# Output projection, second norm and routing in 13 tiles of 125 rows where they were 16 of 100, with attention's result in a ring of 250 columns

## The chip, the cores and the metric

The kernel runs on 1 core of one Trainium2 chip. The metric is device time in microseconds (us); lower is better. Before the change it is 1721.82 us, the median of 3 runs (1720.84 to 1722.42).

## What is computed

A gated cross-attention block and a mixture of experts behind it, for 16 batches (B) of 100 rows (S) of 512 features (D), all in float32:

```python
x = x + tanh(g_xattn) * attention(layernorm(x), ctx)   # 16 heads of 32, 722 context rows per batch
    # q = xn @ Wq.T + bq ; k, v = ctx @ Wk.T + bk, ctx @ Wv.T + bv
    # softmax(q k.T / sqrt(32) + mask) @ v, heads side by side, then @ Wo.T + bo
x = x + tanh(g_ffn) * moe(layernorm(x))
    # gates = softmax(xn @ gate_w + gate_b), the best 2 of 8 experts per row
    # expert: gelu(xn @ w1 + b1) -> gelu(. @ w2 + b2) -> . @ w3 + b3, weighed by its gate
```

From the output projection on, nothing depends on the batch that a row belongs to: projection, residual, norm and routing are done row by row.

## The kernel before, in words

**Precision.** The large products are made of three passes of matmuls: each float32 operand is split into a high and a low part (`PRODUCTS`: high*high, high*low, low*high). ScalarE (ACT) writes the high parts, VectorE (DVE) the low ones.

**Two halves.** The first half of the program (0 to about 999 us) is attention with projection, norm and routing; the second runs the experts over rows that routing has scattered to `expert_in_rows` in HBM. The amount of work in the second half is fixed by constants. Most of one expert (the "early" one, 256 rows) is run in the last part of the first half.

**Bodies.** The first half is a prologue, `first_body` (b = 0), fourteen times `body` (b = 1 to 14; b = 14 is a small variant), and `last_body` (b = 15). All are unrolled, and the order of each engine's work is written by hand. Body b has four groups. Group g computes the scores of the four heads of g (`scores`, line 791), has the softmax run on DVE and ACT (`score` L1470, `exps` L1145), meanwhile finishes the four heads of the group before (`attend`, L814 and L817), runs "units" of filler work on TensorE (PE), and transposes the probabilities (`transpose_probs`, L803) in two pairs. Units are the keys (K, 12 matmuls, L736) and values (V, 12 matmuls of 512 columns, L750) of this and the next batch, the queries (Q, L773), and, once for each body, Y (`project_o`, L830, the output projection of the batch before: 12 matmuls of 512 columns) and CNT (`count_pairs`, L855 and L856, four small matmuls). Units alternate between two PSUM banks; a unit waits until the unit two before it has been read out (`emptied`).

**Attention's result.** After `attend`, `scale_o` on DVE multiplies the bank by the reciprocal sums into `o_t` (L1492). It stands inside `scored_around`, between the second and the third of four `score` instructions. Only at g = 2 (for the three tiles of g = 0, 1, 2 at once, 300 columns) and at g = 3 (100 columns) is `o_t` split into `o_high` (L1497) and `o_low` (L1499).

**The round of a tile.** One round follows each batch, in the next body: Y; on DVE `residual`, `residual_add` with norm statistics, `norm_out`, eight router dots (`dots`, L1535: one for each expert, each of which overwrites its row of router weights, so POOL loads that row again, `load_router`, L543, four slots), `biased`, `less_max`, `choose` (L1559 to L1567), `place`, `carry`, `aim`; on ACT `rstd_start`, `second_copy`, `route_exps`; on POOL `scatter` (L563). SP stores `x_res` (L645) and loads the next (L657). For the last two tiles the logits come from PE instead of the dots. In DVE's program `values_out` of V2 (L1451) stands behind `choose`, and CNT on PE waits for `either` (L1567). In `last_body`, `early_raw` (L1635) on DVE reads out the early expert's first layer, behind the `scored_around` of the group.

**POOL at the start.** POOL fills the experts' regions in HBM with eight DMAs of 3.3 MB (L555), and after five of them issues the first four router loads. Then it follows the dots of tile 0.

## Time and profile before

| | |
|---|---|
| median of 3 runs | 1721.82 us |
| profiled execution, its own time | 1722.78 us |
| its span | 1720.9 us |
| outside the span | 1.88 us |
| PE busy, share of the span | 99% |
| DVE, ACT, POOL | 70%, 54%, 10% |
| granted TensorE clock | full in every slice of the span |
| in the chain that ended last | PE 88%, DVE 2%, ACT 1% |

The profile is of one execution. A row of the timeline gives an instruction's start and its duration; consecutive matmuls overlap in it, so that the time that a group of matmuls takes is the distance from its first start to the first start of what follows. The chain of waits is followed back from the last instruction, at each step to what released it; there the pieces don't overlap and their lengths can be added.

### The profile page before, as it was taken

What the parts mean: (1) busy time and instruction counts of PE and PEld (TensorE: products, weight loads), DVE (VectorE), ACT (ScalarE), POOL (GpSimd) and SP (SyncE); (2) the same over time, 40 slices, a digit from 0 to 9 for tenths busy, and PEclk for the clock granted to TensorE, in tenths of its full rate; (3) what the DMA queues carried; (4) which work ended last, traced back from release to release, by engine and by line L of the source; (5) the groups of instructions that cost most, each with busy time, mean ns of one, the idle gap of its engine ahead of it and who ended that gap; (6) DMA issues with size and microseconds to landing.
All of it is one profiled execution on the core that took longest, in us unless ns stands there. A gap on an engine that the chain in (4) does not pass through costs nothing.

```text
span 1720.9 us, 40335 instructions
## 1 busy us (share of the span) xinstructions
PE 1704.8 (99%) x15462; PEld 1509.2 (88%) x15462; DVE 1209.4 (70%) x2807; ACT 931.6 (54%) x1652; POOL 180.1 (10%) x271
## 2 busy tenths in 40 slices
PE   9999999999999999999999999999999999999997
PEld 8888888898889888988898878777899999999997
DVE  5677777777777777777775575566677777777773
ACT  4655656565556555655555454455545555545551
POOL 2010110111011101110110100000011010110100
PEclk9999999999999999999999999999999999999999
DMA  9982322222222222221215499998666666667662
GB/s 296 371 316 77 83 89 78 66 83 88 67 77 83 88 68 77 83 89 46 80 33 182 174 367 384 348 353 285 200 214 214 212 205 206 209 224 226 219 197 49
DMA packets 128181, 292.72 MB, mean 170 GB/s; under 512 B 19610, under 2 KB 42842, under 8 KB 128040
## 3 DMA queue, kind: packets, MB, share of 16 engines
q1 hardware_dynamic: 104616, 225.46, 38.8%
q0 software_dynamic: 23424, 65.30, 12.8%
q8 instruction: 98, 1.61, 0.4%
q14 instruction: 43, 0.35, 0.1%
HBM read 244.04 MB, written 46.66 MB: 169 GB/s over the span
## 4 chain that ended last, share of the span: by engine, by line
PE 88%; DVE 2%; issue 1%; ACT 1%; DMA 0%; POOLq 0%; POOL 0%; DVEq 0%; ACTq 0%
PE bank_rows L2301 21%; PE bank_rows L750 13%; PE bank_rows L736 12%; PE bank_rows L2316 7%; PE bank_rows L803 6%; PE bank_rows L2355 5%; PE bank_rows L791 4%; PE bank_rows L814 3%; PE bank_rows L2341 3%; PE bank_rows L2382 3%; PE bank_rows L830 2%; PE bank_rows L773 2%; PE bank_rows L894 2%; DVE probs L1470 1%; PE bank_rows L2393 1%
## 5 line engine op out<-in xcount | busy, mean ns | idle before, releaser
L1145 ACT ACTIVATE probs<-probs,neg_max 100x726 f32<-100x726 f32 x256 | 228.9, 896 | 168.1 <-DVE neg_max L1470 168.1
L2545 DVE TENSOR_TENSOR w_low<-stage,w_high 128x1024 fp32r<-128x1024 f32 x176 | 213.3, 1223 | 35.5 <-ACT w_high L2449 35.0
L1470 DVE CUSTOM_DVE_ANT_0 probs<-bank_rows,mask_sb 100x726 f32<-100x726 f32 x256 | 222.9, 909 | 16.4 <-PE bank_rows L791 14.8
L2449 ACT ACTIVATE w_high<-stage 128x1024 fp32r<-128x1024 f32 x176 | 183.9, 1057 | 33.4 <-DMA stage<-in_L_ffn_w 33.2
L2472 ACT ACTIVATE gelu<-bank_rows,biases 128x256 f32<-128x256 f32 x176 | 82.3, 474 | 216.4 <-PE bank_rows L2301 211.7
L1151 ACT ACTIVATE p_t<-bank_rows 122x1200 f32<-122x1200 f32 x128 | 146.4, 1168 | 95.8 <-PE bank_rows L803 95.8
L2301 PE MATMUL bank_rows<-h_high,w_high 128*128 128x256 f32 x704 | 196.5, 279 | 0.0
L2301 PE MATMUL bank_rows<-h_low,w_high 128*128 128x256 f32 x704 | 196.5, 279 | 0.0
L2301 PE MATMUL bank_rows<-h_high,w_low 128*128 128x256 f32 x704 | 196.5, 279 | 0.0
L736 PE MATMUL bank_rows<-ctx_high,wk_high 128*128 128x360 f32 (+1 forms) x512 | 175.7, 343 | 3.3 <-DVE v_even L1451 2.1
L736 PE MATMUL bank_rows<-ctx_low,wk_high 128*128 128x360 f32 (+1 forms) x512 | 167.8, 328 | 0.0
L736 PE MATMUL bank_rows<-ctx_high,wk_low 128*128 128x360 f32 (+1 forms) x512 | 167.2, 326 | 0.0
L750 PE MATMUL bank_rows<-wv_high,ctx_high 128*120 128x512 f32 (+1 forms) x384 | 154.5, 402 | 0.3 <-DVE k_low L1444 0.3
L750 PE MATMUL bank_rows<-wv_high,ctx_low 128*120 128x512 f32 (+1 forms) x384 | 151.4, 394 | 0.0
L750 PE MATMUL bank_rows<-wv_low,ctx_high 128*120 128x512 f32 (+1 forms) x384 | 151.3, 394 | 0.0
L803 PEld LDWEIGHTS bank_rows<-ident,probs 100*120 100x120 f32 (+1 forms) x1536 | 138.8, 137 | 10.3 <-ACT probs L1145 1.4
L803 PE MATMUL bank_rows<-ident,probs 100*120 100x100 f32 (+1 forms) x1536 | 143.8, 249 | 0.2
L2301 PEld LDWEIGHTS bank_rows<-h_high,w_high 128*128 128x128 f32 x704 | 132.3, 188 | 0.0
L2301 PEld LDWEIGHTS bank_rows<-h_low,w_high 128*128 128x128 f32 x704 | 132.3, 188 | 0.0
L2301 PEld LDWEIGHTS bank_rows<-h_high,w_low 128*128 128x128 f32 x704 | 132.3, 188 | 0.0
L1122 ACT ACTIVATE k_high<-bank_rows,bk_sb 128x362 fp32r<-128x362 f32 (+1 forms) x128 | 71.9, 562 | 94.2 <-PE bank_rows L736 93.9
L2559 DVE CAST h_high<-gelu 128x256 fp32r<-128x256 f32 x176 | 51.7, 294 | 99.5 <-ACT gelu L2472 99.5
(245 smaller groups left out, 3869.9 us busy)
## 6 DMA issues: line engine op xcount, KB each, us to landing
stage<-in_L_ffn_w SPq DMA_DIRECT2D x240, 512.0 KB, 4.7
plain_w<-in_L_ffn_w SPq DMA_DIRECT2D x15, 2048.0 KB, 12.4
expert_in_rows<-filling POOLq DMA_DIRECT2D x8, 3341.0 KB, 25.2
router_rows<-in_gate_rows POOLq DMA_DIRECT2D x112, 200.0 KB, 3.4
ctx_raw<-in_ctx SPq DMA_DIRECT2D x16, 720.0 KB, 4.9
ctx_raw<-in_ctx SPq DMA_DIRECT2D x15, 724.0 KB, 4.3
xs_sb<-expert_in_rows SPq DMA_DIRECT2D x11, 514.0 KB, 5.4
b_sb<-in_L_ffn_b SPq DMA_DIRECT2D x19, 256.0 KB, 4.9
```

The lines of the kernel that those rows point to most:

```text
L736: last = nc.tensor.matmul(bank[:, 0:size], wk_hl[a][:, c, m * P:(m + 1) * P], ctx_t[b][half][:, c, :], start=(c == 0 and s == 0), stop=(c ...
L750: last = nc.tensor.matmul(bank[0:rows, :], ctx_t[a][half][:, c, off:off + rows], wv_hl[b][:, c, :], start=(c == 0 and s == 0), stop=(c == ...
L803: last = nc.tensor.transpose(slots_of(q)[0:rows, i // 2, i % 2 * S:(i % 2 + 1) * S], probs[:, q, off:off + rows], ident[0:S, 0:S])
L1145: nc.scalar.activation(p, p, ACT.Exp, bias=neg_max[:, h:h + 1], scale=-1.0, accum_out=exp_sum[:, h:h + 1]).then_inc(probs_ready, 1)
L1151: nc.scalar.activation(p_t[:, q:q + 2, :, :].rearrange("t q (k i) s -> t (q k) (i s)", k=PIECES), slots[0:TT, PIECES * q:PIECES * (q + 2), ...
L1470: nc.vector.tensor_tensor_reduce(out=pieces(probs[:, q, :]), in0=slots_of(q)[0:S, :, 0:PIECE], in1=pieces(mask_sb[:]), scale=-1.0, scalar= ...
L2301: last = nc.tensor.matmul(mm_bank[m % 4][:, 0:BLOCK], w[a][:, k, m * P:(m + 1) * P], src[c][:, k, :], start=(k == 0 and s == 0), stop=(k = ...
L2316: last = nc.tensor.matmul(y_bank[t][:], h_hl[1][a][:, k, t * P:(t + 1) * P], w_hl[2][c][:, k, :], start=(k == 0 and s == 0), stop=(k == HT ...
L2355: last = nc.tensor.matmul(second_bank[half][:], small_h1[a][:, k, :], w_hl[1][c][:, k, cols], start=(k == 0 and s == 0), stop=(k == HT - 1 ...
L2449: nc.scalar.activation(hi, src, ACT.Copy).then_inc(chunk_hi[which], 1)
L2472: nc.scalar.activation(gelu[:, m % 2, :], mm_bank[m % 4][:, 0:BLOCK], ACT.Gelu, bias=bias_of(n, layer, m)).then_inc(g_done, 1)
L2545: nc.vector.tensor_tensor(lo, src, hi.bitcast(F32), ALU.subtract).then_inc(chunk_lo[which], 1)
```

## The change

Rows of batches 0 to 14 (1500 rows) are taken as 12 tiles of 125 rows; batch 15 is tile 12, with 100 rows. A tile is done in the first body after which its rows are complete (`tile_of`): bodies 1, 6 and 11 have none. There Y, CNT and everything of the round on DVE, ACT and POOL are left out, and V4 takes Y's place on PE. The output of attention goes to a ring of 250 columns for each feature tile. A batch that crosses the ring's end (2, 7 and 12) is written in two pieces of 50 columns. `scale_o` splits its own 100 columns at once, for each g. POOL's first router loads come behind all eight region fills, since one of the four slots now lies where `filling` is. Some tensors get another place in SBUF. Tensors of a tile have 125 partitions where they had 100.

```diff
+R = 125
+NR = (B - 1) * S // R + 1
+FIRST_TILES = NR - 2
+RING = 2 * R
+def tile_of(body):
+    if body == B:
+        return NR - 1
+    done, last = (S * b // R for b in (body, body - 1))
+    return done - 1 if done > last else None
+
+def ring_pieces(b):
+    at, first = S * b % RING, min(S, RING - S * b % RING)
+    return [(at, 0, first)] + ([(0, first, S - first)] if first < S else [])
...
+    if 0 < body < B - 1 and tile_of(body) is None:
+        _names = tuple(u for u in _names if u not in ("Y", "CNT"))
...
-    o_hl = [place(f"o_{n}", [P, DT, S], F32R) for n in ("high", "low")]
+    o_hl = [place(f"o_{n}", [P, DT, RING], F32R) for n in ("high", "low")]
...
     (on_gpsimd)
         def load_router(e):
             k = e % ROUTER_SLOTS
-            pool.dma_start(router_rows[k][:], gw_rows[e:e + 1, :].broadcast_to([S, D])
+            pool.dma_start(router_rows[k][:], gw_rows[e:e + 1, :].broadcast_to([R, D])
                            ).then_inc(router_loaded[k], 16)
...
             elif e == len(FILL_AFTER):
                 pool.wait_ge(mask_loaded, 64)
-                for k in range(ROUTER_SLOTS):
-                    load_router(k)
...
-        pass_router(0, E)
         pool.wait_ge(regions_filled, 16 * E)
-        scatter(0)
-        with pool.Fori(1, IN_ROWS - 1) as b:
-            pass_router(b, E)
-            scatter(b)
+        pool.wait_ge(spare_filled, 32 * TPB)
+        for k in range(ROUTER_SLOTS):
+            load_router(k)
+        with pool.Fori(0, IN_ROWS - 1) as t:
+            pass_router(t, E)
+            scatter(t)
...
     (on_sync)
-        def load_after(b, t):
+        def load_after(t):
             stored(t)
-            sp.dma_start(x_res[:], batch_rows(x, b)).then_inc(xres_loaded, 16)
+            sp.dma_start(x_res[0:rows_in(t + 1), :], tile_rows(x_rows, t + 1)).then_inc(xres_loaded, 16)
...
     (on_tensor)
         def project_o(body, cs=range(DT)):
             bank, ready = bank_for(body, "Y", cs[0] == 0)
-            t = body - 1
+            t = tile_of(body)
+            n, at = rows_in(t), R * t % RING
             if cs[0] == 0:
                 pe.wait_ge(wo_split, 2)
-                pe.wait_ge(o_split, 2 * t + 1)
+                pe.wait_ge(o_split, DT * (body - 1) + DT - 1)
             for c in cs:
                 if c == DT - 1:
-                    pe.wait_ge(o_split, 2 * t + 2)
+                    pe.wait_ge(o_split, DT * (body - 1) + DT)
                 for step, (a, w) in enumerate(PRODUCTS):
-                    last = nc.tensor.matmul(bank[0:S, :], o_hl[a][:, c, :], wo_hl[w][:, c, :],
+                    last = nc.tensor.matmul(bank[0:n, :], o_hl[a][:, c, at:at + n], wo_hl[w][:, c, :],
                                             start=(c == 0 and step == 0), stop=(c == DT - 1 and step == 2))
...
         def body(b, odd, t, n):
             scores(b, 0)
-            attend(b, t, 1 - odd, 3)
+            attend(b, b - 1, 1 - odd, 3)
             values(b, 3)
-            project_o(b)
+            if t is not None:
+                project_o(b)
+            else:
+                values(b, 4)
             transpose_probs(b, 0)
             transpose_probs(b, 1)
-            values(b, 4)
+            if t is not None:
+                values(b, 4)
             values(b, 5)
...
-            count_pairs(b, t)
+            if t is not None:
+                count_pairs(b, t)
...
     (on_vector)
         def scale_o(body, b, g):
             bank, done = take(body, f"A{g}")
             dve.wait_ge(r_copied, DT * b + g + 1)
-            nc.vector.tensor_tensor(o_t[:, g, :], bank[:, 0:S], r_sb[:], ALU.mult).then_inc(done, 1)
-            if g >= DT - 2:
-                bank, fills = unit(body, f"A{g}")
-                dve.wait_ge(emptied[bank], fills)
-                gs = slice(0, DT - 1) if g == DT - 2 else slice(DT - 1, DT)
-                nc.vector.tensor_copy(o_hl[0][:, gs, :], o_t[:, gs, :]).then_inc(o_hi, 1)
-                dve.wait_ge(o_hi, 2 * b + g - 1)
-                nc.vector.tensor_tensor(o_hl[1][:, gs, :], o_t[:, gs, :], o_hl[0][:, gs, :].bitcast(F32),
-                                        ALU.subtract).then_inc(o_split, 1)
+            nc.vector.tensor_tensor(o_t[:], bank[:, 0:S], r_sb[:], ALU.mult).then_inc(done, 1)
+            bank, fills = unit(body, f"A{g}")
+            dve.wait_ge(emptied[bank], fills)
+            for at, first, size in ring_pieces(b):
+                nc.vector.tensor_copy(o_hl[0][:, g, at:at + size], o_t[:, first:first + size]).then_inc(o_hi, 1)
+            dve.wait_ge(o_hi, o_pieces_to(b, g))
+            for at, first, size in ring_pieces(b):
+                made = nc.vector.tensor_tensor(o_hl[1][:, g, at:at + size], o_t[:, first:first + size],
+                                               o_hl[0][:, g, at:at + size].bitcast(F32), ALU.subtract)
+            made.then_inc(o_split, 1)
...
         def body(b, odd, t, n):
-            residual(b, t)
-            residual_add(b, t)
+            if t is not None:
+                residual(b, t)
+                residual_add(b, t)
...
-            dots(t, (5, 6, 7))
-            biased(t)
-            less_max(t)
+            if t is not None:
+                dots(t, (5, 6, 7))
+            if t is not None:
+                biased(t)
+                less_max(t)
```

The same `if t is not None` stands before `norm_out`, the other `dots`, `choose`, `place`, `carry` and `aim` on DVE, and before `rstd_start(1, t)`, `second_copy` and `route_exps` on ACT. In `last_body` and behind it the tile is `tile_of(15)` = 11 and then 12. The experts' half only has the counts in its waits changed (16 tiles to `NR` = 13).

## Rows read from the trace of the kernel before

**Rows 1.** The page, busy time by engine (us, share, instructions).

```profile
PE 1704.8 (99%) x15462; PEld 1509.2 (88%) x15462; DVE 1209.4 (70%) x2807; ACT 931.6 (54%) x1652; POOL 180.1 (10%) x271
```

**Rows 2.** Waits of PE, longest in total: waiter, released by, us, times, longest.

```profile
PE bank_rows L736 <- DVE v_even L1451: 2.1, 2, 1.6
...
PE bank_rows L814 <- DVE k_low L1444: 1.1, 1, 1.1
```

**Rows 3.** Chain of waits in body 12: start, us, what.

```profile
733.46 2.77 PE bank_rows L830 x12
736.23 2.06 PE bank_rows L803 x24
738.29 5.60 PE bank_rows L750 x24
```

**Rows 4.** PE's timeline around CNT in body 8: start, us, instruction.

```profile
606.12 2.22 PE L803 MATMUL bank_rows<-ident,probs 100*122 100x100 f32 x24
608.18 0.26 PE L855 MATMUL bank_rows<-either,before 100*100 100x8 f32 x2
...
608.52 0.43 PE L736 MATMUL bank_rows<-ctx_high,wk_high 128*128 128x360 f32 x1
```

**Rows 5.** Windows from one Y to the next: stretch, length, busy times, clock, DMA.

```profile
95.60:156.05 60.45, 58.64 (x643) 51.36 (x642) 43.92 (x125) 34.25 (x67) 6.45 (x10) 1.00 0.70 238
502.43:560.50 58.07, 57.97 (x641) 51.03 (x640) 43.71 (x123) 34.16 (x67) 6.61 (x10) 1.00 0.27 78
618.13:675.83 57.70, 57.70 (x642) 50.92 (x641) 43.71 (x123) 34.17 (x67) 6.61 (x10) 1.00 0.26 79
```

**Rows 6.** Router loads: chain in body 1; DMA issues, median landing; all waits.

```profile
128.08 7.21 DMA router_rows<-in_gate_rows
...
router_rows<-in_gate_rows POOLq DMA_DIRECT2D x112, 200.0 KB, 3.4
...
  DMA router_rows<-in_gate_rows: 14.5, 15
```

**Rows 7.** DVE's timeline, `scale_o` and the score behind it, at g = 3, 1, 2.

```profile
442.71 0.26 DVE L1492 TENSOR_TENSOR o_t<-bank_rows,r_sb 128x100 f32<-128x100 f32 x1 [0.43 <-ACT r_sb L1132]
...
443.44 0.91 DVE L1470 CUSTOM_DVE_ANT_0 probs<-bank_rows,mask_sb 100x726 f32<-100x726 f32 x1
...
473.04 0.26 DVE L1492 TENSOR_TENSOR o_t<-bank_rows,r_sb 128x100 f32<-128x100 f32 x1 [0.44 <-ACT r_sb L1132]
473.22 0.90 DVE L1470 CUSTOM_DVE_ANT_0 probs<-bank_rows,mask_sb 100x726 f32<-100x726 f32 x1
...
486.53 0.26 DVE L1492 TENSOR_TENSOR o_t<-bank_rows,r_sb 128x100 f32<-128x100 f32 x1 [0.44 <-ACT r_sb L1132]
...
487.56 0.91 DVE L1470 CUSTOM_DVE_ANT_0 probs<-bank_rows,mask_sb 100x726 f32<-100x726 f32 x1
```

**Rows 8.** Timelines in group 2 of body 7: V1 read out, next K unit.

```profile
477.18 0.69 DVE L1451 TENSOR_TENSOR v_even<-bank_rows,bv_sb 120x512 f32<-120x512 f32 x1
...
478.72 0.41 PE L736 MATMUL bank_rows<-ctx_high,wk_high 128*128 128x362 f32 x1
```

**Rows 9.** Chain of waits at the end of body 7's group 3.

```profile
491.63 0.18 DVE either L1567
...
492.06 0.70 DVE v_even L1451
...
492.81 4.21 PE bank_rows L736 x24
```

**Rows 10.** PE's timeline, a wait in body 0 and one in body 15.

```profile
60.26 0.50 PE L750 MATMUL bank_rows<-wv_high,ctx_high 128*120 128x512 f32 x1 [0.35 <-DVE k_low L1444]
...
937.15 0.48 PE L878 MATMUL bank_rows<-early_xt,early_w 128*128 128x256 f32 x1 [0.16 <-DVE early_h L1635]
```

**Rows 11.** Timelines of ACT and PE in body 7: last copy, next scores.

```profile
449.88 1.16 ACT L1151 ACTIVATE p_t<-bank_rows 122x1200 f32<-122x1200 f32 x1
...
454.92 0.36 PE L791 MATMUL bank_rows<-k_high,q_high 32*100 32x242 f32 x4
```

More of the change, by code:

```diff
@@ L483, in pieces, with ln_rows @@
         return ap.rearrange("s (k t) -> s k t", k=PIECES)
+    def ln_rows(which, n):
+        return slice(0, S if which == 0 else rows_in(n))
     def early_bank(m):
@@ L706, in load_early @@
                 if which == 1:
-                    store(B - 2)
-                    load_after(B - 1, B - 2)
+                    store(NR - 2)
+                    load_after(NR - 2)
         for b in range(B - 1):
-            body(b, b - 1 if b > 0 else None, b + 1, b + 2 if b + 2 < B else None)
+            body(b, tile_of(b) if b > 0 else None, b + 1, b + 2 if b + 2 < B else None)
         load_early()
-        store(B - 1)
-        stored(B - 1)
+        store(NR - 1)
+        stored(NR - 1)
         sp.wait_ge(spare_filled, 32 * TPB)
@@ L1082, in on_tensor @@
         for b in range(1, B - 1):
[L1083 removed]
+            body(b, b % 2, tile_of(b), b + 1)
         last_body(B - 1, (B - 1) % 2)
@@ L1275, in body @@
             keys_high(b, n, *((1, 0) if odd else (0, 1)))
-            route_exps(t)
+            if t is not None:
+                route_exps(t)
             if b + 2 < B:
@@ L1389, in on_scalar @@
         for b in range(1, B - 1):
-            body(b, b % 2, b - 1, b + 1)
+            body(b, b % 2, tile_of(b), b + 1)
         last_body(B - 1)
@@ L1577, in place @@
+            route_then(t, k + 4, nc.vector.tensor_scalar(token[:], token[:], float(R), None, ALU.add))
         def place(body, t):
@@ L1759, in body @@
             keys_low(b, b, 3, 1)
-            dots(t, (0,))
+            if t is not None:
+                dots(t, (0,))
             if b + 2 < B:
-                ln_apply(0, b + 2, x_ln[:], xn[:], xn_ready)
+                ln_apply(0, b + 2, x_ln[:], xn[0:S, :], xn_ready)
             recips(b, 1)
@@ L1767, in body @@
                 ctx_low(n, 3)
-                dots(t, (1,))
+                if t is not None:
+                    dots(t, (1,))
                 values_out(b, 1 - odd, 0)
-                dots(t, (2,))
+                if t is not None:
+                    dots(t, (2,))
                 keys_low(b, n, 0, 0)
@@ L1775, in body @@
                 ctx_low(n, 3)
-                dots(t, (1,))
+                if t is not None:
+                    dots(t, (1,))
                 keys_low(b, n, 0, 0)
-                dots(t, (2,))
+                if t is not None:
+                    dots(t, (2,))
                 keys_low(b, n, 1, 0)
@@ L1796, in body @@
             keys_low(b, n, 3, 0)
-            choose(t)
+            if t is not None:
+                choose(t)
             values_out(b, 1 - odd, 2)
             recips(b, 3)
-            place(b, t)
-            carry(t)
-            aim(t)
-            if t == FIRST_BATCHES - 1:
+            if t is not None:
+                place(b, t)
+                carry(t)
+                aim(t)
+            if t == FIRST_TILES - 1:
                 pick_early()
@@ L1894, in on_vector @@
         for b in range(1, B - 1):
-            body(b, b % 2, b - 1, b + 1)
+            body(b, b % 2, tile_of(b), b + 1)
         last_body(B - 1)
```

287 lines of the change are left out of this document (158 added, 129 removed).

## The prediction

> **What bounds the kernel now.** I read four views in this order. The page first: PE is busy for 1704.8 of 1720.9 us, so only about 16 us are idle, and PE's own work is what a change has to shorten [rows 1]. Then PE's waits: they are few, and the largest two are for DVE [rows 2]. Then the stretch from one output projection to the next, body by body. An undisturbed body takes 57.70 us with PE busy for all of it, at the full granted clock (2.4 GHz); nine of the twelve from body 2 to 13 lie between 57.63 and 57.73, of which one stands here. Body 1 takes 60.45, body 8 58.07 [rows 5]. Last the chain of waits, which inside an undisturbed body consists of PE's units back to back: 12 matmuls of Y, the transposes, two units V [rows 3]. So a unit that is taken out of a body returns its whole length, as long as nothing that stood in its shadow comes out.
>
> **Three rounds less, on PE.** `tile_of` gives None where S*b//R doesn't grow: 0 at b = 0 and 1, 4 at b = 5 and 6, 8 at b = 10 and 11. So three bodies lose Y and CNT, and 13 rounds stay. Y runs from 733.46 to 736.23, 2.77 us [rows 3]: 3 * 2.77 = 8.31 us. That the other Y have 125 rows in place of 100 costs nothing by the rows: the 12 matmuls of V, with 120 result rows, take 5.60 / 2 = 2.80 us [rows 3], for the same 512 columns. CNT starts at 608.18 and the next unit at 608.52, 0.34 us [rows 4]; 3 * 0.34 = 1.02. The transposes before it take 608.18 - 606.12 = 2.06 [rows 4], the same as those that are followed by V [rows 3], so nothing is hidden in that border. Sum: **-9.33 us**.
>
> What covered what there: Y stood between V3 and the transposes, where the softmax of heads 0 to 3 has to get ready. V4 now takes its place, with the same length, so that cover stays. Behind the transposes two units stood before the next scores, now one. These scores wait for the last copy of the transposed probabilities, which ends at 449.88 + 1.16 = 451.04; they start at 454.92 [rows 11]. Taking 2.77 away leaves 454.92 - 2.77 - 451.04 = 1.1 us. The cover holds.
>
> The round's DVE, ACT and POOL work (some 40 instructions on DVE) also goes three times. I cost that at nothing: PE doesn't wait for it in an undisturbed body.
>
> **Body 1.** It is 60.45 - 57.70 = 2.75 us longer than its kind [rows 5]. The chain leads to a router row that took 7.21 us to land, where the median is 3.4 [rows 6]: the fills of the experts' regions keep the DMA engines busy (share 0.70 in this stretch, 0.26 later [rows 5]). DVE waits in the dots, and the waits of rows 2 are PE's behind it. Body 1 has no tile now, so it has no dots: **-2.75 us**. What is late next? Tile 0 is in body 2, whose dots stand behind its Y; that Y was at 156.05 [rows 5] and comes to about 150. The first four loads now wait for all the fills, which saves POOL the issue of four loads ahead of the last three fills; the DMA share falls from 0.70 over this body to about 0.27 in the later ones, and the router row of the chain landed at 128.08 + 7.21 = 135.3 [rows 6]. Even if the first loads were no earlier than that, they would be there 15 us before Y. Bounds: 0 (another wait takes its place) to -2.75; I take -2.75, since the chain goes through this load alone.
>
> **`scale_o` on DVE.** At g = 3 the step with a split of 100 columns takes 443.44 - 442.71 = 0.73 us from its start to the next score; at g = 1 without a split 473.22 - 473.04 = 0.18; at g = 2 with 300 columns 487.56 - 486.53 = 1.03 [rows 7]. After the change each is like g = 3. So the third and fourth scores come 0.55 us later at g = 0 and 1, and 0.30 earlier at g = 2. With two pieces (batches 2, 7, 12) there are two more short instructions; I estimate 0.2 us more, from an `either` of 0.18 us [rows 9] less the overlap of neighbours. Who waits for that:
>
> - Steady bodies, group 2 (g = 1): the chain on DVE runs on to V1's read-out, which ends at 477.18 + 0.69 = 477.87, and the K unit that needs that bank starts at 478.72: 0.85 us to spare in odd bodies [rows 8]. 0.55 leaves 0.30, and 0.75 in body 7 leaves 0.10. Cost nothing; upper bound 0.2 for each of 14 bodies, 2.8, if a stray pause falls there.
> - Group 3 (g = 2): V2's read-out stands behind `choose`. In body 7 it starts at 492.06 and K starts at 492.81 where it ends [rows 9]: PE waited. This is the excess of body 8 too, 58.07 - 57.70 = 0.37 [rows 5]; three bodies (7, 8, 12) have it, 0.9 us together. 0.30 us earlier takes about half of it: **-0.5 us** (bounds -0.9 and 0).
> - Body 0: PE waited 0.35 us for a `k_low` behind the softmax's scores [rows 10], so there the 0.55 comes through: **+0.5** (0 to 0.8).
> - Body 15: the early expert's first layer waits for `early_raw`, 0.16 us already [rows 10], once behind g = 0 and once behind g = 1. 2 * 0.55 = **+1.1** (0 to 1.7).
>
> **Other queues.** SP has three store-load pairs less and otherwise the order that it had. POOL scatters 125 rows thirteen times for 100 rows sixteen times. The experts' half has the same units. All at nothing: PE waits for none of them in rows 2.
>
> **The sum.** -8.31 - 1.02 - 2.75 - 0.5 + 0.5 + 1.1 = -10.98, say **-11.0 us**. The span goes from 1720.9 to 1709.9. The profiled execution took 1722.78, so its like would take 1711.8. It lay 0.96 above the median of 1721.82, so I forecast a median of **1710.8**.
>
> **A rule that speaks against the change.** A row of router weights lands in 3.4 us with 100 partitions [rows 6]. The Trainium skill, page "DMA: Bandwidth & Descriptors", section "Why a DMA increments its semaphore by 16 and not by 1", says that a DMA is spread over the largest number of engines up to 16 that divides its slowest dimension: 10 for 100 partitions, which by that rule is 5 for 125; it names an exception on trn2, where copies from GpSimd's queue use 16 engines with partitions/16, rounded up, on each. By the exception a router load has 8 rows on an engine where it had 7, and the sum stands; by the rule it takes about twice as long, and the next paragraph's first rival gives the time. No row here shows how many engines a transfer uses.
>
> **Rivals.**
>
> 1. *Router rows for 125 partitions land late (slower).* Dot 4 needs the load that dot 0 released, and so on; DVE waited 15 times for one, 14.5 us in all [rows 6], so this is a live edge in every body. Body 1 shows the price: 7.21 - 3.4 = 3.8 us late cost 2.75 on PE, so the first 1.05 are free. If all loads took 6.8 us, 3.4 late, each of 11 tiles in dots would cost 3.4 - 1.05 = 2.35: +25.9 - 11.0 = +14.9, 1736.7. It decides from a landing of 5.4 us, at which the 11.0 are used up (1.0 a tile). Against it: 250 KB for 200 is a quarter more of what is mostly a fixed time.
> 2. *The splits come through everywhere (slower).* 0.55 in two groups of 14 bodies is 15.4: -11.0 + 15.4 = +4.4, 1726.2. It decides from 11.0 / 28 = 0.4 us a group. Against it: 0.85 to spare [rows 8].
> 3. *Body 1 stays slow.* Something else waits for the crowded DMA engines: -8.2, 1713.6. The mask, context and x loads of body 1 share them, but the chain names none.
> 4. *The cover of the three short bodies fails* and PE waits for the softmax instead: -11.0 + 9.33 = -1.7, 1720.1. Against it: the 1.1 us above.
> 5. *The change doesn't do what it says*, the rounds aren't fewer or their units remain: also about 1720. The schedule worked out above speaks against it.
>
> **How the numbers follow.** Forecast 0.79, rival 1 0.03, rival 2 0.03, rival 3 0.10, rival 4 0.03, rival 5 0.02. The bounds of the forecast: all stalls gone and none added, -12.98, 1708.8; every upper bound taken, -8.31 - 1.02 - 2.75 + 0.8 + 1.7 + 2.8 = -6.8, 1715.0. This takes in rival 3. The runs of before spread over 1.6 us, so I add 0.8 at either end: 1708.0 to 1715.8. A difference under 0.2% (3.4 us) can't be told from none. Faster by more than that: 0.79 + 0.10 = 0.89; within it: 0.05; slower: 0.06.
>
> **What would show it.** 156 matmuls of Y in place of 192; the windows of bodies 6 and 11 near 54.6 us; body 1 also near 54.6; PE's waits for L1451 near 2 us gone; `o_high` with 128x100 in most rows; router rows landing near 3.5 us. I'm wrong if the other bodies rise above 57.8, if PE waits for `v_even`, `v_odd` or `early_h` in many bodies, or if a wait in body 1 goes to another DMA.

## The result and the profile after

| | before | after |
|---|---|---|
| median, 6 runs each | 1721.78 us | 1729.05 us |
| lowest and highest | 1720.84, 1722.42 | 1725.84, 1730.16 |
| profiled execution, its own time | 1722.78 us | 1729.57 us |
| its span | 1720.9 us | 1727.8 us |

The ratio is 1.004 with a 95% interval of 1.0027 to 1.0052: slower by 7.3 us where 11.0 us less was forecast. PE's busy time fell, as in [rows 1]; the page of after:

```profile
PE 1703.0 (99%) x15414; PEld 1512.8 (88%) x15414; DVE 1187.2 (69%) x2754; ACT 932.4 (54%) x1637; POOL 167.4 (10%) x241
```

So less work took longer. The waits of PE in after (columns as in [rows 2]), and DVE's waits for the three transfers that matter:

```profile
PE bank_rows L842 <- ACT probs L1193: 4.8, 1, 4.8
PE bank_rows L880 <- DVE x L1482: 3.2, 1, 3.2
PE bank_rows L775 <- DVE v_even L1507: 1.8, 1, 1.8
...
DVE router_rows L1595 <- DMA router_rows<-in_gate_rows: 11.4, 11, 1.6
...
DVE probs L1526 <- DMA bo_sb<-in_L_xattn_bo: 8.2, 1, 8.2
...
DVE rstd L1472 <- DMA expert_in_rows<-x,pair_row: 4.2, 1, 4.2
```

The first two waits of PE are new. L842 is the transposes of the first probabilities in body 0, L880 the transposes of x2 in the last stretch (tile 11). Behind each stands a DVE step that waits for a DMA. The first one, in the chain of waits of after (start, us, what):

```profile
28.66 18.01 DMA bo_sb<-in_L_xattn_bo
46.89 0.92 DVE probs L1526
47.85 1.88 ACT probs L1193 x4
49.78 4.26 PE bank_rows L842 x24
```

In before, DVE's first scores start at 37.79 us. In both kernels one wait, for all of `gw_sb`, `gb_sb` and `bo_sb`, stands ahead of body 0 on DVE (`dve.wait_ge(small_loaded, 16 * 3)`). The windows show what PE does meanwhile (stretch, length, busy times, clock, DMA share, GB/s):

```profile
40.00:50.00 10.00, 5.17 (x24) 3.77 (x23) 3.11 (x7) 2.15 (x5) 1.20 (x1) 0.94 0.47 153
50.00:60.00 10.00, 10.00 (x64) 8.93 (x67) 5.19 (x12) 4.56 (x9) 1.15 (x1) 0.72 1.02 366
```

PE idles for 4.8 us, and after it the granted clock is 0.72 in the next stretch, between the levels of 1.2 and 2.4 GHz. The first scores of body 1 start at 100.80 us, where they were at 90.48. The second new wait, in the same chain:

```profile
956.71 6.47 DMA expert_in_rows<-x,pair_row
...
963.20 0.23 DVE rstd L1472
...
963.84 0.56 DVE x L1482
...
964.53 0.90 PE bank_rows L880 x4
965.43 3.46 PE bank_rows L936 x8
```

`rstd` opens the last step of tile 11's norm, which writes `x2`; it may not do so before the scatter of tile 10 has read that buffer. In before this wait is 1.1 us, behind other work. Here PE stops for 3.2 us, and the granted clock is 0.55 in the 10 us from 964.76 on: the 8 matmuls above take 3.46 us, at full clock 1.75 (in the version with `gb_sb` and `bo_sb` below, whose clock did not fall there).

**Where the 6.9 us of span come from.** I cut both spans at three points: the first scores of body 1 (90.48 and 100.80 in PE's timelines), Y of tile 0's round in body 2 (156.05 and 160.72), and Y in body 15 (917.37 and 914.76).

| stretch | before | after | difference |
|---|---|---|---|
| start to the scores of body 1 | 90.48 | 100.80 | +10.3 |
| from there to Y in body 2 | 65.57 | 59.92 | -5.7 |
| Y in body 2 to Y in body 15 | 761.32 | 754.04 | -7.3 |
| Y in body 15 to the end | 803.53 | 813.04 | +9.5 |
| span | 1720.90 | 1727.80 | +6.9 |

The gain is there, 13.0 us of it; 19.8 us were lost at the two ends. In the middle the windows are as good as forecast (columns as in [rows 5]; bodies 2, then 5 and 6 together, of which one has no Y, then 8):

```profile
160.72:218.43 57.71, 57.71 (x641) 51.24 (x641) 44.85 (x135) 34.41 (x67) 6.79 (x10) 1.00 0.31 89
...
333.80:445.92 112.12, 112.12 (x1265) 99.73 (x1265) 76.74 (x206) 67.66 (x128) 6.81 (x10) 1.00 0.22 64
...
503.55:561.31 57.76, 57.76 (x642) 51.23 (x641) 44.60 (x127) 34.63 (x67) 6.81 (x10) 1.00 0.32 90
```

**The theory.** The transfers that grew from 100 to 125 partitions use fewer of the 16 DMA engines, because 125 has no larger divisor up to 16 than 5, where 100 has 10. Windows of 1 us over the last scatters ahead of the wait, before and then after (the two columns at the end are the DMA share and GB/s):

```profile
958.00:959.00 1.00, 1.00 (x6) 0.90 (x5) 0.87 (x2) 0.00 (x0) 0.80 (x1) 1.00 0.56 148
959.00:960.00 1.00, 1.00 (x6) 0.87 (x6) 0.82 (x3) 0.00 (x0) 0.00 (x0) 1.00 0.57 148
```

```profile
958.00:959.00 1.00, 1.00 (x6) 0.88 (x5) 0.82 (x3) 0.15 (x1) 0.00 (x0) 1.00 0.30 87
...
961.00:962.00 1.00, 0.33 (x2) 0.00 (x0) 0.00 (x0) 0.00 (x0) 0.00 (x0) 1.00 0.28 109
```

10 of 16 engines would be a share of 0.63, 5 of 16 one of 0.31; the rows show 0.56 and about 0.3. The same share stands at the start of after, shortly before `bo_sb` lands at 46.67 us, when other transfers have run dry:

```profile
38.00:40.00 2.00, 2.00 (x40) 1.70 (x41) 0.69 (x1) 1.51 (x2) 0.00 (x0) 1.00 1.01 340
...
44.00:46.00 2.00, 0.95 (x5) 0.40 (x3) 0.00 (x0) 0.00 (x0) 0.00 (x0) 1.00 0.33 123
```

This was read after the result, so it had to be tried. The width can't be all of the 18.01 us: at the 123 GB/s of the second row the 504 KB of `x_res`, `gb_sb` and `bo_sb` would take about 4 us (an estimate). From 32 to 40 us the DMA engines are busy throughout (share 1.01 and more), and POOL issued a region fill of 3.3 MB at 28.40 us. How much of the delay is the company of that fill isn't shown: no run was made without it.

### The profile page after: what moved, and what is told of

It reads as the page before. It is cut to its first block, busy times and chain, and to the rows that moved or that the text cites. A ratio compares the mean times of both kernels' runs of the same rounds, so it can differ in the third digit from the quotient of the medians.

```text
span 1727.8 us, 40017 instructions
## 1 busy us (share of the span) xinstructions
PE 1703.0 (99%) x15414; PEld 1512.8 (88%) x15414; DVE 1187.2 (69%) x2754; ACT 932.4 (54%) x1637; POOL 167.4 (10%) x241
## 4 chain that ended last, share of the span: by engine, by line
PE 94%; DMA 2%; DVE 1%; SPq 1%; ACT 1%; issue 1%; POOL 0%; POOLq 0%; DVEq 0%; ACTq 0%
PE bank_rows L2382 21%; PE bank_rows L789 15%; PE bank_rows L775 14%; PE bank_rows L842 7%; PE bank_rows L2397 7%; PE bank_rows L2436 5%; PE bank_rows L830 4%; PE bank_rows L853 4%; PE bank_rows L2422 3%; PE bank_rows L2463 3%; PE bank_rows L812 2%; PE bank_rows L870 2%; PE bank_rows L936 1%; DMA bo_sb<-in_L_xattn_bo 1%; PE bank_rows L856 1%; PE bank_rows L2474 1%
## 5 line engine op out<-in xcount | busy, mean ns | idle before, releaser
L842 PEld LDWEIGHTS bank_rows<-ident,probs 100*120 100x120 f32 (+1 forms) x1536 | 140.4, 139 | 15.2 <-ACT probs L1193 6.9
L842 PE MATMUL bank_rows<-ident,probs 100*120 100x100 f32 (+1 forms) x1536 | 145.8, 251 | 5.0 <-ACT probs L1193 4.8
L1500 DVE SCALAR_TENSOR_TENSOR k_low<-bank_rows,bk_sb,k_high 128x362 fp32r<-128x362 f32 (+1 forms) x128 | 75.7, 593 | 74.9 <-ACT k_high L1170 74.4
```

The costliest lines, as they stand in the source:

```text
L842: last = nc.tensor.transpose(slots_of(q)[0:rows, i // 2, i % 2 * S:(i % 2 + 1) * S], probs[:, q, off:off + rows], ident[0:S, 0:S])
```

## The experiments

Each time is a median beside runs of the kernel before on the same chip, and each ratio is to that. Three chips were used. On one ran `bo_sb` alone, the scatter alone, all four at 128 and the longer cover (kernel before: 1727.6 us), and later the kernel before, its version with loads of 125, the wait moved and 127 rows (1728.5). On another ran the unedited changed kernel, `x_res` alone, `gb_sb` and `bo_sb`, and all three loads (1727.3); on a third the last three (1728.9). For the result above the kernel before took 1721.8 us. On which chip that was isn't known, so that the chip makes this difference is likely and not shown.

Lines left out of an edit are marked by dots or follow from its first lines.

**bo_sb alone.** The chain names `bo_sb`, so its load got 128 rows:

```
-    bo_sb = place("bo_sb", [R, D])
+    bo_sb = place("bo_sb", [P, D])
...
-        sp.dma_start(bo_sb[:], spread(bo, R)).then_inc(small_loaded, 16)
+        sp.dma_start(bo_sb[:], spread(bo, P)).then_inc(small_loaded, 16)
```

> The changed kernel with one edit: bo_sb is loaded into 128 partitions in place of 125. Theory 'few engines': a transfer over 125 partitions runs on few DMA engines and so lands late (18.0 us for bo_sb in the changed kernel's chain, behind which PE stood idle for 4.8 us at the start and its clock fell for some 20 us). Then bo_sb lands soon enough, the wait of DVE's first scores of batch 0 goes from 8.2 us to under 2 and the time falls by 5 to 10 us, to 1719 to 1724; less if gb_sb or x_ln, also in that queue, is next. Rival 'more bytes': 128 partitions are more bytes than 125, so nothing improves, 1729.

Measured: 1730.68 us, 1.0011 (1.0001 to 1.0021), for 1719 to 1724 expected, and DVE's wait was still there:

```profile
DVE probs L1526 <- DMA bo_sb<-in_L_xattn_bo: 8.2, 1, 8.2
```

That is a miss: the load that the chain names isn't the cause of its own lateness.

**The scatter alone.** `x2` and `pair_row` have 128 rows; the last three are zeros that go to rows behind the table, which nothing reads. The scatter of the last tile keeps its 100 rows.

```
-    x2 = place("x2", [R, 2, ROW])
+    x2 = place("x2", [P, 2, ROW])
...
-    pair_row = place("pair_row", [R, 2], U32)
+    pair_row = place("pair_row", [P, 2], U32)
...
-        def scatter(t, n=R):
+        def scatter(t, n=P):
...
-            scatter(t, rows_in(t))
+            scatter(t, P if t < NR - 1 else S)
```

> The changed kernel with each scatter of a tile of 125 rows padded to 128 rows; the three more go to rows of HBM that nothing reads. Theory 'few engines': tile 11's scatter, which took 6.5 us from issue to landing and held up the norm of tile 12 and with it PE (3.2 us and a clock of 0.55 for 10 us behind it), lands in about 3 us; the DMA share while one scatter runs goes from about 0.3 to 0.6 or more; the stretch from the last but one Y to the first small expert shrinks by 6 to 8 us, the time to 1721 to 1723. Rival 'more bytes': landing stays at 6.5 us or more and the time at 1729.

Measured: 1724.81 us, 0.9982 (0.9972 to 0.9991). DVE's wait ahead of the last `rstd` is 0.8 us in place of 4.2, and PE's at the transposes is gone. Against the version with `bo_sb` alone on the same chip, which has the same end as the unedited kernel, that is 5.9 us less; the end itself (Y in body 15 to the end) takes 804.59 us for 813.05, 8.5 less in the profiles, for 6 to 8 expected. Why the medians give less follows behind the last experiment.

**All four at 128 rows.** The scatter as above, `bo_sb`, `gb_sb` and `x_res` too (rows 125 to 127 of `x_res` are the next tile's; nothing reads them there).

```
-        sp.dma_start(x_res[:], tile_rows(x_rows, 0)).then_inc(xres_loaded, 16)
+        sp.dma_start(x_res[:], x_rows[0:P, :]).then_inc(xres_loaded, 16)
...
-            sp.dma_start(x_res[0:rows_in(t + 1), :], tile_rows(x_rows, t + 1))
+            rows = P if t + 1 < NR - 1 else S
+            sp.dma_start(x_res[0:rows, :], x_rows[R * (t + 1):R * (t + 1) + rows, :])
```

> The changed kernel with bo_sb, gb_sb, x_res and the scatter all on 128 partitions. Theory 'few engines' for both the start and the tail: both losses go, and what stays is the gain that was forecast for PE, 9.3 us of units and 2.8 of body 1, less 1 to 2 us of later scores: 1710 to 1713. Rival: the gain isn't there at all and the losses only hid it partly: 1718 or more.

Measured: 1714.93 us, 0.9926 (0.9909 to 0.9943). This beats both kernels. It is over the 1710 to 1713 expected, where the kernel before is 5.8 us slower than at the result. Neither wait is left; the one for the scatter is 0.5 us, and DVE's first scores start at 37.20 us.

**A longer cover at the end.** Nothing of the transfers is touched; in TensorE's order of the last stretch, the transposes of x2, the router's product and CNT come one unit of the early expert later.

```
+            early_second(2)
             transpose_x2(b + 1, t + 1)
-            early_second(2, range(0, HT // 2))
+            early_second(3, range(0, HT // 2))
...
```

> The changed kernel with PE's order in the tail changed: the transposes of tile 12's norm, the logits and the counts each stand one unit of the early expert's second layer (3.5 us) later. The scatter itself is as slow as in the changed kernel. Theory 'exposed wait plus clock': PE has work while it waits, 3.2 us of idle time and the fall of the clock behind it go together, so the time falls by 6 to 8 us, to 1721 to 1723; DVE still waits about 4 us for the scatter. Rival 'the slow scatter crowds the DMA engines' and delays loads of the experts' half: the time stays near 1729.

Measured: 1726.96 us, 0.9993 (0.9983 to 1.0003). DVE waits for the scatter as long as before (4.3 us), PE doesn't: its clock stays at 1.00 from 956 us on. The gain is 3.7 us against the version with `bo_sb` alone on the same chip, about half of the 6 to 8 expected. It doesn't show that the stop itself was the price: the end takes 808.09 us, 3.5 more than with the scatter repaired (804.59). The table behind the last experiment shows where that comes from.

**The changed kernel again**, unedited.

> The changed kernel once more, unedited, as the yardstick of this chip: on the chip of the four runs so far the kernel before took 1727.6 us and not 1721.8, so the edited kernels have to be read against an unedited one there. If the two kernels move together from chip to chip, it is 1.004 of the kernel before, with DVE's first scores held by the load of bo_sb until about 46 us, the scatter's wait of about 4.2 us ahead of the last rstd, and a span some 7 us over that of the kernel before. If the loss hung on the first chip alone, the ratio is at or below 1.

Measured: 1730.33 us, 1.0012 (1.0002 to 1.0021), with waits of 10.1 us (`bo_sb`) and 4.2 us (scatter). The loss is there, but the kernel before is 5.5 us slower here and this one only 1.3 us. The profile of the kernel before, below, looks into that, on another of the three chips.

**x_res alone**: only the edit of `x_res` above.

> The load of x_res at the start (and in every body) takes 128 rows for 125; bo_sb and gb_sb stay at 125. Theory A, one long transfer on few of the engines is what delays all that is queued behind it, and that is x_res, the first of the three: the first scores move from about 46 to about 38 us and the time falls by about 9 us against the unedited changed kernel. Theory B, every load whose rows are 125 is late by itself and the wait counts all of them: the first scores stay at 44 to 46 us and the time moves by under 2 us, as it did when bo_sb alone was widened.

Measured: 1722.47 us, 0.997 (0.9959 to 0.998), 7.9 us less than unedited, for about 9 expected. DVE's wait is 2.9 us and its first scores start at 39.56:

```profile
DVE probs L1527 <- DMA bo_sb<-in_L_xattn_bo: 2.9, 1, 2.9
```

So `x_res` makes most of the delay and not all of it; with `gb_sb` and `bo_sb` at 128 as well (all three loads, below) no wait for `bo_sb` is left.

**gb_sb and bo_sb**, `x_res` left at 125.

```
-        sp.dma_start(gb_sb[:], spread(gb, R)).then_inc(small_loaded, 16)
-        sp.dma_start(bo_sb[:], spread(bo, R)).then_inc(small_loaded, 16)
+        sp.dma_start(gb_sb[:], spread(gb, P)).then_inc(small_loaded, 16)
+        sp.dma_start(bo_sb[:], spread(bo, P)).then_inc(small_loaded, 16)
```

> gb_sb and bo_sb take 128 rows, x_res stays at 125. Theory A (x_res in front delays the rest): no gain, first scores at 44 to 46 us, as with bo_sb alone. Theory B (each load by itself, and the wait counts gw_sb, gb_sb and bo_sb alone): the first scores come at about 38 us, and the time falls by about 9 us.

Measured: 1730.17 us, 1.0016 (1.0006 to 1.0025), DVE's wait 8.6 us. No gain. Theory A holds: a transfer for which nobody waits at that time (`x_res` is first read in body 2) makes the ones behind it late.

**All three loads**, the scatter at 125.

> All three loads (x_res, gb_sb, bo_sb) take 128 rows; the scatter stays at 125. With both causes at work side by side, the one at the start is gone and the one at the end stays: first scores at about 38 us, the scatter's wait of 4.2 us still there, time between the unedited changed kernel and the version with all four widened, about 9 us under the former and 5 to 8 us over the latter (1714.9 us where the kernel before took 1727.6). If the start alone were the cause, it equals the version with all four widened within 1 us.

Measured: 1720.2 us, 0.996 (0.9947 to 0.9972). That is 10.1 us under the unedited 1730.33. With the scatter repaired, the same three loads are worth 1724.81 - 1714.93 = 9.9 us on the other chip: the gain at the start doesn't depend on the end, so the two causes add up.

**The kernel before, profiled on the chip of the first four.**

> The kernel before itself, profiled on the chip of the runs so far, where its median was 1727.3 to 1727.6 us and not 1721.8. If the 5.5 us more come evenly from its bodies, the spacing of its output projections is above 57.66 us here; if they come at the start, the first one of body 1 stands after 97 us. Either way the first scores stand near 38 us and the scatter's wait near 1.1 us, and the ratio is 1.000.

Measured: 1728.78 us, 1.000 (0.999 to 1.0009). The chain of waits has its Y at 155.24 in body 2's place and 922.41 in body 15, 767.17 us apart for 761.32. So it is the bodies that are longer here, by 0.45 us each (5.85 in 13). V2's read-out is in the chain in bodies 7, 8 and 12 alone, as in the profile of before [rows 9]. What differs is a pause of PE in a body's last scores, here in body 10 (start, us, what):

```profile
672.89 1.05 PE bank_rows L791 x11
673.94 0.04 issue
673.99 0.58 PE bank_rows L791 x8
```

In the profile of before the same place in the chain is one piece:

```profile
670.39 1.23 PE bank_rows L791 x32
```

The profile names nothing that PE waited for, and the cause stays open. The changed kernel has less of it: unedited, it takes 757.52 us from Y in body 2 to Y in body 15 (on the chip of the group above) for 754.04 in the result, 3.5 us more, where the kernel before has 5.9 more.

**The kernel before with loads of 125.** Only the first loads of `x_res`, `gb_sb` and `bo_sb` take 125 rows, 25 of them for nobody.

```
-        sp.dma_start(x_res[:], x[0]).then_inc(xres_loaded, 16)
+        sp.dma_start(x_res[:], x.rearrange("a s d -> (a s) d")[0:125, :]).then_inc(xres_loaded, 16)
-        sp.dma_start(gb_sb[:], spread(gb, S)).then_inc(small_loaded, 16)
-        sp.dma_start(bo_sb[:], spread(bo, S)).then_inc(small_loaded, 16)
+        sp.dma_start(gb_sb[:], spread(gb, 125)).then_inc(small_loaded, 16)
+        sp.dma_start(bo_sb[:], spread(bo, 125)).then_inc(small_loaded, 16)
```

> The kernel before with nothing of the change except the width of its three loads at the start: x_res, gb_sb and bo_sb take 125 rows for 100 (the 25 more are read by nobody). If 125 rows at the start are a cause by themselves, without the new tiling, DVE's first scores move from about 38 to 44 to 47 us and the time rises by 7 to 10 us (ratio 1.004 to 1.006). If the loss needs the rest of the change (bodies without an output projection, the ring), the first scores stay at 38 us and the ratio is within 0.001 of 1.

Measured: 1735.14 us, 1.0038 (1.0026 to 1.0049), 6.6 us slower with the same work, a little under the 7 to 10 expected:

```profile
DVE probs L1470 <- DMA bo_sb<-in_L_xattn_bo: 9.7, 1, 9.7
...
PE bank_rows L803 <- ACT probs L1145: 6.4, 1, 6.4
```

The width of these loads is a cause by itself, with none of the new tiling.

**The wait moved.** The changed kernel with its transfers as they are, DVE's wait ahead of body 2 in place of body 0.

```
-        dve.wait_ge(small_loaded, 16 * 3)
...
         for b in range(1, B - 1):
+            if b == 2:
+                dve.wait_ge(small_loaded, 16 * 3)
```

> The changed kernel with all transfers as they are, but DVE's wait for the three small loads moved from ahead of body 0 to ahead of body 2, whose output projection is the first that needs them. If the loss at the start is this wait, the first scores stand at 38 to 40 us and the time is 8 to 10 us under the unedited changed kernel's 1730.3 us (1720 to 1722), like the version with the three loads widened (1720.2 us). If the slow transfer holds back what is queued behind it too (the next x_ln and context), part of that comes back as another wait in bodies 0 and 1, and the gain is 2 to 6 us.

Measured: 1729.71 us, 1.0003 (0.9994 to 1.0013). DVE's first scores are at 37.30 us again, and almost nothing is won:

```profile
DVE stats L1459 <- DMA x_ln<-in_x: 14.9, 2, 12.4
PE bank_rows L775 <- DVE v_even L1507: 11.2, 2, 10.3
```

The chain of waits shows the same:

```profile
30.24 25.12 DMA x_ln<-in_x
```

The next input behind in the queue, x of batch 1, took 25.12 us from its issue, and PE waited 10.3 us in one piece (in the profiled run, which at 1733.20 us was the longest of ten). The gain is 0.6 us by the medians of two chips and about 1.6 by the ratios, for 2 to 6 expected in this case.

**127 rows.** The version with all four at 128, but the first load of `x_res` and the scatters of tile 11 with 127, a prime.

```
+        sp.dma_start(x_res[0:127, :], x_rows[0:127, :]).then_inc(xres_loaded, 16)
+            scatter(t, (P, 127, S)[t - IN_ROWS + 1])
```

> All four transfers at 128 rows, except two that take 127: the load of x_res at the start and the second-last tile's two scatters. A DMA's engines by the widest divisor up to 16 would be one for 127 rows, against five for 125 and ten for 100. In that case both delays are far above those at 125: from the 98 GB/s at a share of 0.28 that the end of a 125-row load in a body showed, one engine moves about 22 GB/s, so that 254 KB take 11.5 us alone: first scores at 55 us or later, and a wait of 12 us or more ahead of the last rstd, the time at 1740 us or over. If what matters is only whether the rows are a multiple of 16, the two waits equal those at 125: first scores at about 39 us (as with 125 rows in x_res and bo_sb at 125 they stood at 46) and a wait of about 4.3 us, time 1718 to 1727 us.

Measured: 1751.72 us, 1.0126 (1.0107 to 1.0146), about 35 us over the version at 128 (1.0126 for 0.9926), for a row less in three DMAs. SP's timeline at the start (start, us, instruction) and DVE's waits:

```profile
22.97 1.80 SPq L676 DMA_DIRECT2D x_res<-in_x  x1
24.82 16.16 SPq L677 DMA_DIRECT2D gw_sb<-in_L_ffn_gate_w  x1
...
DVE probs L1533 <- DMA bo_sb<-in_L_xattn_bo: 15.2, 1, 15.2
...
DVE rstd L1479 <- DMA expert_in_rows<-x,pair_row: 20.1, 1, 20.1
```

A window while nothing but the scatter runs:

```profile
984.00:985.00 1.00, 0.00 (x0) 0.00 (x0) 0.00 (x0) 0.00 (x0) 0.00 (x0) 0.50 0.07 25
```

A share of 0.07 is one engine of 16 (0.0625), at 25 GB/s. At the start the share falls to 0.08, at 28 GB/s, from 42 to 44 us. In the profiles Y in body 2 comes 14.2 us later than with all four at 128, and the stretch from Y in body 15 to the end is 22.4 us longer. The wait ahead of `rstd` is above the 12 us expected for one engine, and the time above the 1740 us. The first scores came at 51.48 us, a little before the 55 expected. SP's issue of the next load, `gw_sb`, took 16.16 us, and `bo_sb`, issued at 44.33, landed 6.9 us later: with 127 rows what was delayed was SP itself. With 125 rows it was the landing: SP issued `bo_sb` at 28.66 us, 0.9 later than in before, and it took 18.01.

**The order.** The changed kernel, no width touched; one statement stands lower.

```
-        sp.dma_start(x_res[:], tile_rows(x_rows, 0)).then_inc(xres_loaded, 16)
         sp.dma_start(gw_sb[:], gw.rearrange("(t p) n -> p t n", p=P)).then_inc(small_loaded, 16)
...
             sp.dma_start(out[B * S:, :][at, :], filling[:, 0, 0:D]).then_inc(spare_filled, 16)
+        sp.dma_start(x_res[:], tile_rows(x_rows, 0)).then_inc(xres_loaded, 16)
```

> The changed kernel with one statement moved: the load of x_res of tile 0 (125 rows still) is issued behind the small loads, x_ln and the filling copies, and not ahead of them; no width is touched. If a transfer over few engines hurts by what is queued behind it, the first scores come earlier than 46 us: by 12.8 us (33.9 against 46.7) less what bo_sb, still over 125 rows, costs, so 38 to 42 us as with x_res at 128 rows, and the time is 5 to 9 us under the unedited changed kernel (1730.3 us on this chip). If the total of bytes on those engines decides, whatever their order, the first scores stay at 44 to 47 us and the time within 2 us.

Measured: 1720.82 us, 0.9952 (0.9937 to 0.9967). DVE's wait is 1.9 us and its first scores are at 37.92 us. The time is 9.5 us under the unedited 1730.33, a little more than the 5 to 9 expected. It is the order that counts: the same bytes over as few engines, issued behind what is needed first, cost next to nothing at the start.

**The cover on top of all four at 128**, and that version again beside it.

> The version with all four transfers at 128 rows, and in TensorE's order of the last stretch the transposes of x2, the router's product and the count of pairs one unit of the early expert later. With the scatter repaired, no wait is left for the later place to cover (0.5 us on DVE, none on PE), so the gain is 0 to 1 us on 1714.9 us; if the later place pushes the last scatter and the early expert's end behind it, it is 1 to 2 us slower.

> The version with all four transfers at 128 rows again, for the comparison with the run before it on the same chip, and for whether it beats both kernels in more rounds: ratio 0.9926 within 0.001 of the kernel before on a chip where that takes 1727 to 1729 us, or 0.9945 to 0.996 (7 to 9 us less) on one where it takes 1721.8.

Measured: 1720.15 us, 0.9948 (0.9935 to 0.9962) with the cover, and 1716.11 us, 0.9927 (0.9914 to 0.9941) without. The cover that gained 3 to 4 us against the slow scatter costs 4.0 us once the scatter is repaired, more than the 1 to 2 expected; the version without repeats its 0.9926. Both timelines of POOL at the last tile's scatter, with the cover first:

```profile
969.69 1.00 POOL L605 DMA_INDIRECT expert_in_rows<-x,pair_row  x1 [17.32 <-DVE pair_row L1667]
```

```profile
966.00 1.00 POOL L605 DMA_INDIRECT expert_in_rows<-x,pair_row  x1 [13.93 <-DVE pair_row L1666]
```

The last scatter goes out 3.7 us later. The chains of both kernels run from it to a load of an expert's weights, issued at 981.33 us with the cover and at 977.57 without, and behind that PE waits with the cover where the experts' half begins:

```profile
PE bank_rows L2430 <- ACT gelu L2586: 2.4, 1, 2.4
...
PE bank_rows L2430 <- DVE small_x L2687: 0.9, 1, 0.9
```

**What the end hangs on.** The first scatter of the last tile (`DMA_INDIRECT` in POOL's timeline) and the end of the span, both from Y in body 15, with PE's stop ahead of the transposes and the clock in the 10 us behind that place:

| version | PE's stop | clock | last tile's scatter | the end |
|---|---|---|---|---|
| kernel before, at the result | none | 1.00 | 55.28 | 803.53 |
| all four at 128 | none | 1.00 | 56.45 | 804.92 |
| longer cover, scatter at 125 | none | 1.00 | 59.87 | 808.09 |
| longer cover, all four at 128 | none | 1.00 | 59.88 | 808.89 |
| `gb_sb` and `bo_sb` | 3.3 | 1.00 | 59.90 | 808.60 |
| unedited, second time | 3.2 | 0.66 | 63.16 | 811.88 |
| unedited, at the result | 3.2 | 0.55 | 64.35 | 813.04 |

The last two columns differ by 748.2 to 749.0 us in every row: the end follows the last scatter. PE's stop puts that off by about 3.4 us, and the cover by as much, so the cover takes away only what the clock adds. And the clock adds between nothing and 4.5 us for the same stop: in the third row from below it never fell. The piece behind the stop in that version's chain, for the 3.46 us in after:

```profile
965.28 0.53 PE bank_rows L880 x4
965.82 1.75 PE bank_rows L936 x8
```

The ten single runs of the unedited kernel fit that, four at 1726.8 to 1727.3 us and six at 1730.3 to 1731.9, and so do the ten with the cover, all at 1726.8 to 1728.0.

## Why the prediction was wrong, step by step

**The step that failed** is "Other queues ... All at nothing: PE waits for none of them in rows 2", and in it the sentence on POOL's scatters and SP's loads of other sizes. The waits of before say what was late then, not what a changed transfer makes late. What it left out was two terms, both put at 0. At the start, `x_res`, `gb_sb` and `bo_sb` over 125 partitions: +10.3 us to the scores of body 1 (shown from both sides: 10.1 us come back when they take 128 rows in the changed kernel, 6.6 us are lost when they alone take 125 in the kernel before). At the end, the scatter over 125: +9.5 us, of which the forecast had 1.1 there, so 8.4. In the experiments the end was 811.88 for 803.89, +8.0 us in profiles on two chips, and the repair gave 7.0 there (804.92), though 5.3 to 5.9 in the medians: the part of the loss that the lower clock makes isn't there in every execution (the table above).

The text had the rule at hand and used it on the wrong transfers. Its paragraph on a rule that speaks against the change looked at the router's rows alone and set the rule against its exception there. The router's rows landed in 3.6 us for 3.4 [rows 6], as the forecast had it, and DVE's waits for them fell from 14.5 to 11.4 us. The question to ask was which transfers of SP and which indirect scatters change their row count too, and who stands behind them in the queue.

As measured here, a scatter of 2 KB rows shows the share of 5 engines at 125 rows, about that of 10 at 100, and that of one at 127. The Trainium skill, page "DMA: Bandwidth & Descriptors", section "Why a DMA increments its semaphore by 16 and not by 1", states the rule, the largest divisor up to 16, with 10 for 100 and 1 for 127 as examples; by that rule, the trace agrees. It adds that transfers issued by SP take the lowest-numbered engines. That would put `x_res` and `bo_sb` on the same five; no run here shows which engines they were.

**A reading that was wrong.** For body 1 the text took the waits of rows 2 as PE's behind the router row. Of the 2.1 us for `v_even` 1.56 stand at 23.40 us, ahead of body 0, and only 0.59 in body 1; with the 1.1 for `k_low` at 137.50 that makes 1.7. So the sign "PE's waits for L1451 near 2 us gone" couldn't come: after still has 1.8 us, at 23.60. What was in body 1 is gone, and nearly all of its 2.75 us with it. PE's timeline of before at the three places:

```profile
23.40 0.40 PE L736 MATMUL bank_rows<-ctx_high,wk_high 128*128 128x360 f32 x1 [1.56 <-DVE v_even L1451]
...
130.94 0.43 PE L736 MATMUL bank_rows<-ctx_high,wk_high 128*128 128x362 f32 x1 [0.59 <-DVE v_even L1451]
...
137.50 1.24 PE L814 MATMUL bank_rows<-p_t,v_odd 122*32 122x100 f32 x48 [1.12 <-DVE k_low L1444]
```

**The steps that held.** Three rounds less: 9.33 us forecast, and the two pairs of bodies with one Y take 112.12 and 112.18 us, so a body without takes 54.4 to 54.5 in place of 57.7, 3.2 to 3.3 each for 3.11. Body 1: -5.7 from its scores on, where its round and its router wait were put at 3.11 + 2.75 = 5.86. The middle: -7.3 for 2 * 3.11 + 0.5 = 6.7; the excess of bodies 7, 8 and 12 went nearly whole (body 8 has 57.76 above, for 58.07 [rows 5]), so that step is near its bound of 0.9. Cover of the short bodies (rival 4), the splits (rival 2) and a still slow body 1 (rival 3): PE has no wait that says so, and no other body rose over 57.8. For body 0 (+0.5) and body 15 (+1.1) PE's own waits grew as forecast, from 0.35 to 0.88 us and from 0.16 to 0.52 and 0.62, in after:

```profile
PE bank_rows L920 <- DVE early_h L1704: 1.1, 2, 0.6
PE bank_rows L789 <- DVE k_low L1500: 0.9, 1, 0.9
```

Their stretches can be read only where the transfers are repaired: against the kernel before on the same chip, the scores of body 1 come 0.85 us later (90.87 for 90.02, the second matmul of each), of which 0.08 stem from the start, for +0.5 forecast; from Y in body 15 to the end it takes 804.92 us for 803.89, +1.0 for +1.1.

**The sum with the failed step mended.** With all four transfers at 128 rows the kernel is 12.7 us under the one before (1714.93 and 1727.62), or 12.8 in the second comparison. The slower bodies there give 2.1 of that: from Y in body 2 to Y in body 15 it saves 767.17 - 757.79 = 9.4 us there, where the changed kernel saved 7.3 at the result; PE's unexplained pauses in the last scores are fewer in the new loop. That leaves about 10.6, beside the 11.0 forecast. No run of it stands beside the kernel before at 1721.8 us. The same pauses, 2.4 us of them, are about half of why the unedited change is 1.004 at the result and 1.0012 in the experiments; the rest is open.

No rival had this. Rival 1 was the same mechanism on a transfer that turned out to be spared; its chance of 0.03 was given from the size of the transfer alone.

## What to carry to other kernels

When rows per tile change, list every DMA whose partition count changes, on all queues, with the largest divisor up to 16 of the old and of the new count, and who is queued behind each: 125 rows for 100 halved the engines though they carried more, and three padding rows in four transfers gave 15 us back in all (1.0012 to 0.9926). A late transfer's cause can be an earlier one in its queue for which nobody waits; moving one load down was worth about 10 us (1.0012 to 0.9952) without touching a width. A wait is priced where PE stops, with the clock behind it, and by what it puts off further on, here the last scatter. A cover puts that off too, so it is too long once the slow transfer is repaired.

## What the runs showed of the hardware

- One transfer can block the issuing queue: with `x_res` over 127 rows SP's next DMA instruction took 16.16 us, for 0.62 with 128 rows. In the changed kernel the load of `x_ln` behind these three took 6.05 us to issue; the kernel before, in the second row, took 0.43, and the version with all four at 128 rows 0.45 (timelines of SP).

```profile
30.43 6.05 SPq L675 DMA_DIRECT2D x_ln<-in_x  x1
```

```profile
28.85 0.43 SPq L636 DMA_DIRECT2D x_ln<-in_x  x1
```

- One DMA engine moved 25 GB/s of scattered 2 KB rows (share 0.07), and indirect scatters of GpSimd show about the same share as the loads of SP at 125 rows (0.28 to 0.30, and 0.33) and at 127 (0.07 and 0.08); its direct loads of router rows showed no loss at 125 partitions (3.6 us for 250 KB).
- A stop of PE of 3.2 us at the end was followed by a stretch of 10 us at a granted clock of 0.55; in another execution a stop of 3.3 us at the same place was followed by 10 us at 1.00. With 4.8 us at the start it was 0.72. In the version at 128 rows it is 1.00 in both places.
- The kernel before was 0.3 to 0.4% slower on each of the three chips of the experiments than at the result, in the one profiled there by 0.45 us a body, by pauses of PE in a body's last scores for which the profile names no wait. A difference of 0.3% was therefore only read against the kernel before on the same chip.
